# Spreading the steps of a two-layer kernel: fewer empty steps at a batch's end, and another weight total for the fronts

## The reference, cut to what matters

```
x = x + L0(groupnorm(x))   # 3x3 local attention, 4 heads, plus 9-tap kernels made per pixel, projection
x = x + L1(groupnorm(x))   # offsets om = conv3x3(x) (27 channels); at each of 9 taps a bilinear
                           # sample of 4 neighbours, times sigmoid(mask); then a 256 x 2304 matmul
```

## Time and profile before

| | |
|---|---|
| median of 3 runs | 5265.98 us (5261.78 to 5272.94) |
| profiled execution | 5259.85 us, span of its instructions 5258.0 us |
| PE busy | 4852.3 us, 92% |
| VectorE busy | 4391.8 us, 84% |
| ScalarE, GpSimd busy | 2248.3 us, 2266.2 us, 43% each |
| PE clock granted, mean | 0.978 |
| DMA | 1451.46 MB, mean 276 GB/s |

### The profile page before, as it was taken

The page is one execution under the profiler, slowest core; times in us unless marked ns, Lnnn a source line. Parts: engine busy times, 40 slices in busy tenths (PEclk is TensorE's granted clock), DMA queues, the critical chain, the costliest instruction groups (busy, mean ns, idle before and its releaser), DMA issues. The chain is left out here.

```text
span 5258.0 us, 79746 instructions
## 1 busy us (share of the span) xinstructions
PE 4852.3 (92%) x26576; PEld 2634.5 (50%) x26576; DVE 4391.8 (84%) x11226; ACT 2248.3 (43%) x5360; POOL 2266.2 (43%) x2311
## 2 busy tenths in 40 slices
PE   7878998999999999999999999899999999998787
PEld 4545554555544555455544555455554555543343
DVE  5748888788997888888898888888888788988888
ACT  2244444344443444434444444434444344443444
POOL 0004444444444444444454444444444444445665
PEclk9989999999999999999999999999999999999899
DMA  5437788877797778977888787888789878798998
GB/s 168 146 135 243 256 277 315 278 260 275 265 345 258 268 268 275 327 252 272 273 295 311 256 276 269 302 287 278 258 275 318 276 261 273 266 326 323 358 365 313
DMA packets 493249, 1451.46 MB, mean 276 GB/s; under 512 B 47524, under 2 KB 117548, under 8 KB 492588
## 3 DMA queue, kind: packets, MB, share of 16 engines
q0 software_dynamic: 331776, 1208.11, 66.5%
q1 hardware_dynamic: 161068, 238.27, 12.9%
HBM read 1309.60 MB, written 136.59 MB: 275 GB/s over the span
## 5 line engine op out<-in xcount | busy, mean ns | idle before, releaser
L762 POOL DMA_INDIRECT G<-table,IDX x2304 | 2265.3, 983 | 2952.7 <-DVE V L1414 2123.4
L781 PE MATMUL ps<-VT,s_wconv 128*128 128x512 f32 x4608 | 2283.0, 619 | 97.7 <-issue 53.6
L1414 DVE SCALAR_TENSOR_TENSOR V<-G,WT,V 128x256 f32<-128x256 f32 x4608 | 2019.0, 479 | 122.9 <-DVE V L1414 2.7
L1142 ACT ACTIVATE VT<-ps 128x512 f32<-128x512 f32 x1152 | 686.9, 596 | 2430.9 <-PE ps L988 1894.4
L781 PEld LDWEIGHTS ps<-VT,s_wconv 128*128 128x128 f32 x4608 | 827.5, 194 | 921.2 <-issue 877.0
L1407 DVE SCALAR_TENSOR_TENSOR V<-G,WT 128x256 f32<-128x256 f32 x2304 | 1007.0, 478 | 234.6 <-ACT G L1131 97.7
L988 PEld LDWEIGHTS ps<-s_ident,V 128*128 128x128 f32 x4608 | 574.2, 143 | 736.2 <-issue 731.5
L1162 DVE TENSOR_TENSOR E<-ps,s_band 128x512 f32<-128x512 f32 x1024 | 649.4, 681 | 271.6 <-PE ps L843 194.7
L1131 ACT ACTIVATE G<-G,WT 128x256 f32<-128x256 f32 x1836 | 825.2, 498 | 26.7 <-DMA G<-table,IDX 16.4
L988 PE MATMUL ps<-s_ident,V 128*128 128x128 f32 x4608 | 705.5, 276 | 75.8 <-DVE V L1414 57.4
L819 PE MATMUL ps<-XN,s_wqk 128*128 128x512 f32 x1024 | 488.2, 605 | 19.5 <-ACT XN L1044 17.7
(11 more groups left out here) (101 smaller groups left out, 2668.6 us busy)
## 6 DMA issues: line engine op xcount, KB each, us to landing
table<-E SPq DMA_DIRECT2D x256, 256.0 KB
G<-table,IDX POOLq DMA_INDIRECT x2304
X<-in_x SPq DMA_DIRECT2D x64, 512.0 KB
x<-X SPq DMA_DIRECT2D x64, 512.0 KB, 5.5
R<-x SPq DMA_DIRECT2D x64, 512.0 KB
out<-R SPq DMA_DIRECT2D x64, 512.0 KB
G<-in_x SPq DMA_DIRECT2D x56, 512.0 KB, 4.1
s_wconv<-in_wconv SPq DMA_DIRECT2D x1, 2304.0 KB, 8.6
```

What stands on the lines that cost most here:

```text
L762: e.indirect_dma_start(G[a % NG][:, :], None, T[b % 2], bass.IndirectOffsetOnAxis(ap=IDX[:, col:col + 1], axis=0)).then_inc(d_g[a % NG], 16)
L781: mm = e.matmul(CV[oh][:, :], s_wconv[:, h, t, oh * P:(oh + 1) * P], VT[U % 2][:, h, :], start=(t == 0 and h == 0), stop=(t == 8 and h == 1))
L1142: e.activation(VT[U % 2][:, :, 2 * P * pair:2 * P * (pair + 1)], BK[banks.place[use]][:, :].rearrange("p (h n) -> p h n", h=2), ACT.Copy). ...
L1414: e.scalar_tensor_tensor(vt[:, :], gt[:, q * C:(q + 1) * C], WT[:, col, q:q + 1], vt[:, :], ALU.mult, ALU.add).then_inc(lerp[q - 1], 1)
```

## The change

Six edits in `order_of_steps`; no instruction is added or taken away, only their order changes.

- For batches after the first, one idle step instead of three behind each norm step and behind the first `pd`, one instead of eight ahead of the last projection, none instead of one behind the norm, and 1 + 1 instead of 1 + 3 ahead of each `pv` of the last chunk.
- Behind `soft.mix` of chunk 7 three idle steps instead of five, in every batch.
- Behind each placing of the last chunk one idle step (four in all), in every batch.
- Ahead of each `ot` in its stream one idle step, so that the next chunk's `tp` comes ahead of it.
- `total` is the weight of the front of batch 1, for all batches.

```diff
--- before.py
+++ after.py
@@ -39,6 +39,7 @@
 ADD = 2
 LAST = 8
 HOP = 3
+NEXT = 1
 CHAIN = 5
 COLLECT, TURN = 3, 2
 NFIRST, NCONST = 9, 8
@@ -96,12 +97,13 @@
 
     def norm(j, b):
 
+        n = NEXT if j == 1 and b > 0 else HOP
         if j == 1:
             yield ("n.aggr", j, b)
-            yield from hop(HOP)
+            yield from hop(n)
         for kind in ("n.mean", "n.dev", "n.var", "n.root", "n.fin"):
             yield (kind, j, b)
-            yield from hop(HOP)
+            yield from hop(n)
 
     def stats1(b):
 
@@ -138,7 +140,7 @@
             yield from hop(CHAIN)
         for kind in ("soft.max", "soft.exp", "soft.mix", "soft.turn", "soft.out"):
             yield (kind, b, c)
-            yield from hop(CHAIN if kind == "soft.mix" and c in (0, NCH - 2, NCH - 1) else 0)
+            yield from hop(CHAIN if kind == "soft.mix" and c in (0, NCH - 2) else HOP if kind == "soft.mix" and c == NCH - 1 else 0)
 
     def last_scores(b, c):
 
@@ -147,7 +149,7 @@
         yield from soften(b, c)
 
     def mix(b, c):
-        alone = HOP if c == NCH - 1 else 0
+        alone = 0 if c < NCH - 1 else HOP if b == 0 else NEXT
         if c < NCH - 1:
             yield from soften(b, c)
         else:
@@ -160,6 +162,8 @@
                 yield IDLE
             for of in (OWN, BORDER):
                 yield ("sel", b, c, of, hp)
+
+                yield from hop(NEXT if c == NCH - 1 else 0)
         for hp in range(2):
             yield from hop(1 + alone)
             yield ("pv", b, c, hp)
@@ -209,10 +213,11 @@
         if b == 0:
             yield from alternate(hop(LAST), norm(0, 1))
         else:
-            yield from hop(LAST)
+            yield IDLE
         yield from project(b, NCH - 1)
         yield from norm(1, b)
-        yield IDLE
+        if b == 0:
+            yield IDLE
 
     def offsets(b, c):
         if c + 1 < NCH:
@@ -234,7 +240,7 @@
 
         before = iter(())
         yield ("pd", b, 0)
-        yield from hop(HOP)
+        yield from hop(HOP if b == 0 else NEXT)
         for c in range(NCH):
             beside = [qkv(b + 1, 0)] if c == NCH - 2 and b + 1 < NB else []
             yield from alternate(offsets(b, c), before, *beside)
@@ -249,10 +255,15 @@
         offsets_run[0] = False
 
     steps = list(begin())
-    n = len(steps)
     steps += list(front(0))
     weigh = lambda s: max(WEIGHT.get(s[0], 0), LEAST)
-    total = sum(weigh(s) for s in steps[n:] if s[0][:3] != "st1")
+
+    sets = (have_kv, have_logits, have_x1)
+    before = [set(v) for v in sets]
+    total = sum(weigh(s) for s in front(1))
+    for v, old in zip(sets, before):
+        v.clear()
+        v.update(old)
     for b in range(NB):
         fr = front(b + 1) if b + 1 < NB else iter(())
         done = 0
```

## The result

Medians of six runs each, in turn on one chip: 5245.2 us after (5236.22 to 5255.27), 5266.83 before (5261.78 to 5272.94), a ratio of 0.996 with an interval of 0.9948 to 0.9971. That is 21.6 us faster where 42.5 were forecast: the direction and the range held, the size is half.

A forecast was written before the change was run, and what follows sets the result against it. PE was taken to set the pace over most of a host batch, VectorE ahead in pairs 88 to 104. Terms 25.5 + 12 + 7 - 21 + 19 = 42.5 us gave 5224 us, range 5190 to 5265.

The forecast's parts named there:

- The idle step ahead of `ot`: At the turned offsets of chunks 3, 4 and 7, PE's waits for their copy would go: 25.5 us gained.
- The placings: In chunk 7, one placing an opening spares PE waits for the bands: 1.75 us a batch, 12 us gained.
- The norm: In the last chunk's norm, `n.mean` waits less, 7 us gained; closer crossings between engines bring new waits, 21 us lost.
- the rival of the table load: Square root's table load and root fall exposed between `n.root` and `n.fin`: 10 us more, 5234 us; chance 0.12.
- the slower one: Six steps of norm and first `pd` each stall an engine and lower PE's clock: 12 us a batch, 5286; chance 0.12.
- The pairs that move: 6.6 empty pairs a host batch move beside other work, mostly where PE sets the pace: 19 us gained.
- price of an empty pair: A pair with nothing beside it costs 2.75 us, against 2.16 where PE sets the pace: 0.59 us each.
- waits only move: Gathers and VectorE take up the offset waits in pairs 105 to 119: net 4 us, 5262, no change; chance 0.12.
- test for being wrong: Forecast wrong if, among other signs, the body's shifted steps get new waits of 4 us or more a batch.
- other signs: Profile after: `soft.mix` of chunk 7 to first `pd` 51 to 56 us, pairs 139 to 142 at 4, batches 621 to 627.

The follow-up runs named there:

- ot_alone: The kernel before with one idle step ahead of each `ot`, total held at 2992: 5216.28 us against 5263.88, ratio 0.9912.
- ot_sel: ot_alone plus one idle step behind each placing of the last chunk, total still 2992: 5144.69 us against 5152.63 before, ratio 0.9983.
- again_before: The kernel before, unchanged, run again on a chip where before takes 5149.66 us: 5148.81 us, ratio 0.9999.
- again_after: The changed kernel with all six edits, run again on a chip where before takes 5149.66 us: 5129.94 us, ratio 0.9958.
- again_steps: The changed kernel with total held at 2992, on a chip where before takes 5149.41 us: 5158.89 us, ratio 1.0018.
- steps_alone: The changed kernel with total held at 2992, so all idle-step edits at the old pace: 5230.48 us against 5263.88 before, ratio 0.9941.
- lead34: The changed kernel with LEAD 34 instead of 30, each step up to one opening earlier: 5130.9 us against 5152.63 before, ratio 0.9954.
- ot_lead34: ot_alone with LEAD 34 instead of 30: 5127.64 us against 5149.41 before, ratio 0.9955.
- again_lead34: The changed kernel with LEAD 34 instead of 30, run again on another chip: 5127.8 us against 5149.41 before, ratio 0.9959.
- total_alone: The kernel before with only total taken from the front of batch 1, 2932 instead of 2992: 5334.91 us against 5263.88, ratio 1.014.

## Why the prediction was right in its direction and wrong in its size

*The idle step ahead of `ot`: 25.5 us.* Right in its mechanism: the waits went from 27.5 to 1.2 us. Alone it was worth 47.6 us on the first group and 21.2 on the second, so the term was sized well for one group and at half for the other. Where the first group's other 22 us come from is settled in part: by the traces pairs 105 to 109 gain 31.4 us there and 19.8 on the second group, since the late start at pair 107, though still in the trace, costs ot_alone no more than it takes on the second group. In the profiled executions the host batches lose 31.9 us of idle time and 4.5 of busy time; of the waits' 27.5 us, 4.3 lie in the front of batch 0, so some 9 us of the idle time were others than these.

*The placings: 12 us.* The waits of 0.96 and 2.52 us and the slow contraction behind them are gone at pair 93 in each batch, as forecast. The term then took this for time won, and that failed. New waits stand close by, 2.5 us at pair 89 and 2.5 at 94, each with its own slow contraction. In ot_sel, this edit on top of ot_alone, the placings' gain turned into waits of `ext`, and the time rose by 12 us.

*The norm: 7 less 21.* `n.mean` waits 1.43 us a batch instead of 3, and `n.var` 0.55, PE's timeline from 2730 us:

```profile
2737.12 0.35 PE L808 MATMUL ps<-mv,s_g 128*128 128x2 f32 x2 [1.43 <-issue]
...
2740.29 0.35 PE L808 MATMUL ps<-gnt,s_g 128*128 128x2 f32 x2 [0.55 <-DVE gnt L1257]
```

and VectorE stands 0.27 us for the square root, from the same place:

```profile
2743.08 0.17 DVE L1268 RECIPROCAL gn<-gnt 128x2 f32<-128x2 f32 x1 [0.27 <-ACT gnt L1045]
```

The gain is 1.7 us a batch by these rows, 11.7 instead of 7, and the losses 0.55 and 0.27 a batch, 6 instead of 21. The gain is one of the first group alone: on the second, `n.mean`'s waits are 8.5 us in all in again_before and 12.7 in again_after. The load of the square root took its 1.28 us from 2741.24, ahead of its operand, and the root followed at 2742.85, 0.33 us behind the load's end, when VectorE's addition was there; of the 1.38 us that the prediction set beside the load the trace shows nothing, since the row ahead of it ends at 2741.21. So the rival of the table load didn't come, nor the slower one (the chain's new waits are far under 9 us a batch).

*The pairs that move: 19 us.* This is the step that failed, and the placings' 12 us with it. Its price of an empty pair holds, 2.74 us between transposes and 20.7 against 18.7 us at the five empty pairs of again_steps. But it took the pairs as moving and all other steps as meeting what they met before. The prediction named that shift as one that it could not price, and in its sum it stands at nothing: whatever changes the total moves all other steps against the pairs. The rest of the change beside the `ot` step was to bring 12 + 7 - 21 + 19 = 17 us. It cost 0.48 points, 25 us, on the first group (after against ot_alone) and nothing, 0.02 points, on the second. So on both groups the 17 us are not there. On the second group the swap of waits accounts for it. On the first, pairs 66 to 71 with their late start cost 41 us more than on the second, and ot_alone loses only some 21 us there at its own, at pair 98: that is most of the 25 us by which the two groups differ in after against ot_alone. The waits at pairs 22, 89 and 94 stand on both groups and are no reason for that difference. The new total alone, by 2% of pace, cost 71 and 97 us.

That 21.6 us came out at half of the forecast has luck in it: on the first group the `ot` step brought 22 us more than its term and the rest 42 us less, and the two misses partly cancel. Of the rivals the nearest is "waits only move", with 4 us, but not by its mechanism: it had gathers and VectorE take up the offset waits, and ot_alone shows that these were time.

The prediction's test for being wrong, new waits of 4 us or more a batch in the body, is met: 2.3, 2.9, 2.6 and 2.5 us at four places. Its other signs held: the stretch from `soft.mix` of chunk 7 to the first `pd` was to take 51 to 56 us and took 52.9, and pairs 139 to 142 slowed down from 2.9 to 4.4 us. So what was reckoned from the edits' own places came, and the loss lies in the body. The host batches came to 603 to 636 us instead of 621 to 627.

Shown is that the pace and the place of the list alone, with no step changed, move the time by 0.2 to 1.8 points. That the new waits are how it does so is read from the traces, and no run took one of them away alone; steps_alone, which has none of the four, is 0.19 points faster than after on the first group and 0.6 slower on the second. Open are what makes ScalarE and VectorE start late on the first group, and 10 of the 22 us that ot_alone brings more there.

Of all versions the one-line ot_alone at the old pace is the best on the first group (0.9912) and equal to after, lead34 and ot_lead34 on the second (0.9954 to 0.996).

## What to carry to other kernels

In one hand-written list for all engines an edit has two effects: the local one, which can be read from the waits around it, and the shift of all that follows, which can cost as much. Hold the pace (here `total`) while a local edit is measured, and try the pace by itself; here the edit with one line gained more than the six together on the first group, and as much on the second. Don't add up single waits as time won: read what came up behind them. Where steps of two streams may meet in one opening, look for a copy that stands behind another copy on ScalarE with no pair's transposes between it and its reader.

## What the runs showed of the hardware

- In a PE that is otherwise full, single waits of 2.5 to 3 us were followed by a contraction of 3.3 to 3.5 us instead of 1.88, at a granted clock of 0.54 to 0.59 (after, pairs 66, 89 and 94). It is no fixed rule: in after the contraction right behind a wait of 2.3 to 3.1 us took over 2.7 us in 16 cases of 21, and in before, behind one of 1.0 to 1.3 us, in 3 of 15. Busy time for the same 23036 matmuls ran from 4122 us (again_lead34) to 4204 us (total_alone).
- Chips of one type differ: the same kernel takes 5264 us or 5150, the gathers of the last batch run at 358 or 395 GB/s, and with an edit the ratio can change its sign (0.9941 and 1.0018).
- On the first group ScalarE and VectorE start together and late at recurring pairs, by waits that the profile marks "remote"; on the second there are none. At pair 66 of after, in all seven host batches, ScalarE's copy started 5.5 to 6.0 us after the last of 48 small matmuls that it reads, and on the second group, in again_after, 0.05 to 0.08 us after it. In host batch 3 the matmuls' run ends at 2575.8, and the transposes that read the copy start at 2582.47. The cause is open.
